# Loads spread over the attention's steps, x prepared group by group, and two reorderings of VectorE and GpSimd work

## The reference

```
# layer 0
xn = x * rsqrt(mean(x*x) + 1e-6);  q, k, v = split(xn @ w_qkv.T, 3)
q, k = rope(q), rope(k)                    # [x1*cos - x2*sin, x2*cos + x1*sin]
a = softmax(where(0 <= i - j <= 32, q k^T / 8, -1e9)) v
x = layernorm(x + a @ w_out.T);  x = layernorm(x + relu(x @ W1 + b1) @ W2 + b2)
# layer 1
k = k / norm(k);  A = tril(k k^T, -1) + I;  u = solve_triangular(A, v, lower=True)
x = layernorm-ed sum of x, (q k^T)(lr * u) @ out_w + out_b, and relu(ln(x) @ w1 + b1) @ w2 + b2
out = layernorm(x + light(x) + heavy(x of the 128 best tokens by coordinate descent))
```

## Time and profile before

| | us |
|---|---|
| median of 3 runs | 504.74 (504.71 to 506.62) |
| profiled execution | 509.57 |
| its span | 507.8 |
| PE / DVE / ACT / POOL busy | 399.8 / 321.9 / 255.8 / 179.1 |
| attention (first scores to end of its last output) | 22.9 to about 235 |
| delta stage | about 268 to 383 |
| MLP | about 383 to 413 |
| routing, feed-forwards, last norm | about 413 to 507.8 |

### The profile page before, as it was taken

The page is one execution under the profiler, slowest core; times in us unless marked ns, Lnnn a source line. Parts: engine busy times, 40 slices in busy tenths (PEclk is TensorE's granted clock), DMA queues, the critical chain, the costliest instruction groups (busy, mean ns, idle before and its releaser), DMA issues.

```text
span 507.8 us, 16578 instructions
## 1 busy us (share of the span) xinstructions
PE 399.8 (79%) x6608; PEld 351.6 (69%) x6608; DVE 321.9 (63%) x1552; ACT 255.8 (50%) x642; POOL 179.1 (35%) x194
## 2 busy tenths in 40 slices
PE   2778799999999999968998402999995668999940
PEld 1667698898998989956785302998983445787840
DVE  2688777777777777867258692222129961688845
ACT  3356545655665656655538300454401464678547
POOL 2733444545444444433535480000006780000004
PEclk9999999999999999999999855899997975999865
DMA  8378855556556465530200403000000000000002
GB/s 258 84 182 226 256 139 134 131 124 145 119 128 145 108 150 134 120 82 3 84 1 0 94 1 93 2 1 1 0 3 0 1 0 1 1 2 2 1 2 83
DMA packets 28861, 38.58 MB, mean 76 GB/s; under 512 B 8368, under 2 KB 20784, under 8 KB 28656
## 3 DMA queue, kind: packets, MB, share of 16 engines
q1 hardware_dynamic: 28496, 36.47, 29.4%
q10 hardware_dynamic: 288, 1.05, 0.5%
HBM read 8.93 MB, written 3.28 MB: 24 GB/s over the span
## 4 chain that ended last, share of the span: by engine, by line
PE 62%; DVE 15%; issue 6%; ACT 5%; POOL 4%; DMA 4%; SPq 3%; POOLq 0%; ACTq 0%; DVEq 0%
PE QK L545 9%; PE VY L618 5%; PE O L596 4%; PE S L572 4%; PE PT L582 3%; PE O L687 3%; PE QK L877 3%; PE PT L605 2%; DVE keys_T L1094 2%; PE QK L751 2%; PE O L759 2%; DMA t_swap<-t_sin 2%; SPq L460 2%; PE QK L857 2%; DVE unread_tests L1204 2%
## 5 line engine op out<-in xcount | busy, mean ns | idle before, releaser
L1516 POOL TENSOR_TENSOR qk<-t_cos,t_swap 128x512 f32<-128x512 f32 x64 | 80.3, 1275 | 110.3 <-DMA t_swap<-t_sin 100.1
L1293 ACT ACTIVATE probs<-probs,negative_max 128x64 f32<-128x64 f32 x256 | 68.0, 338 | 40.2 <-DVE negative_max L948 40.2
L939 DVE TENSOR_TENSOR t_cos<-QK,cos 128x512 f32<-128x512 f32 x64 | 43.9, 687 | 28.4 <-POOL qk L1516 16.2
L948 DVE CUSTOM_DVE_ANT_0 probs<-S,masks 128x64 f32<-128x64 f32 x256 | 39.5, 220 | 8.3 <-PE S L572 8.3
L939 DVE TENSOR_TENSOR t_sin<-QK,sin 128x512 f32<-128x512 f32 x64 | 43.6, 681 | 0.0
L1553 POOL TENSOR_TENSOR rstd<-var_eps,minus_half 128x4 f32<-128x4 f32 x24 | 25.3, 1055 | 37.6 <-DVE var_eps L992 32.8
L1314 ACT COPY oT<-PT 128x512 f32<-128x512 f32 x32 | 18.7, 584 | 38.3 <-PE PT L605 38.3
L545 PE MATMUL QK<-xnT,wq 128*128 128x128 f32 x256 | 36.1, 286 | 1.3 <-ACT xnT L1324 0.7
L618 PE MATMUL VY<-wo,oT 128*128 128x128 f32 x256 | 34.8, 279 | 1.3 <-ACT oT L1314 0.7
L596 PE MATMUL O<-v_before,probsT 64*32 64x65 f32 x1024 | 29.0, 225 | 8.7 <-issue 7.0
L545 PE MATMUL QK<-xnT,wk 128*128 128x128 f32 x256 | 35.1, 282 | 0.6 <-DVE t_sin L939 0.6
(11 more groups left out here) (272 smaller groups left out, 1098.8 us busy)
## 6 DMA issues: line engine op xcount, KB each, us to landing
t_swap<-t_sin SPq DMA_DIRECT2D x128, 128.0 KB
v_before<-v_own SPq DMA_DIRECT2D x32, 132.0 KB
v_before<-v_own SPq DMA_DIRECT2D x62, 66.0 KB
late_tile<-late_weights SPq DMA_DIRECT2D x1, 1513.0 KB, 7.6
x_sb<-x SPq DMA_DIRECT2D x4, 256.0 KB, 5.9
inverse_dram<-invT SPq DMA_DIRECT2D x1, 1024.0 KB, 5.1
gram_dram<-gram SPq DMA_DIRECT2D x4, 256.0 KB, 2.3
invT<-inverse_dram SPq DMA_DIRECT2D x4, 256.0 KB, 5.5
```

What stands on the lines that cost most here:

```text
L939: last = nc.vector.tensor_tensor(dst[:, u % G, PAIRS * j:PAIRS * j + PAIRS], QK[j][:].rearrange("p (m t) -> p m t", m=PAIRS), table[:, tok ...
L948: last = nc.vector.tensor_tensor_reduce(out=probs[:, u % G, m, e, :], in0=S[:, e, m, :], in1=masks[:, min(u // G, 1), :], scale=-1.0, scal ...
L1293: last = nc.scalar.activation(probs[:, u % G, m, e, :], probs[:, u % G, m, e, :], ACT.Exp, scale=-1.0, bias=negative_max[:, u % G, e, m:m ...
L1516: nc.gpsimd.tensor_tensor(qk[:, h, c, WINDOW:WINDOW + P], t_cos[:, h, c], t_swap[:, h, c], ALU.add).then_inc(rope_done, 1)
```

## The change

1. SyncE's loads. x's group 1 is loaded at the start, groups 2 and 3 in steps 4 and 12. The rope tables for tokens 512 and up come in three pieces of 512 tokens in steps 1, 9 and 17. late_tile comes in eight pieces in steps 9, 11, ... 23, and the five smaller loads in steps 24 to 26. wv and the second piece of the tables are issued earlier; wo is issued between the swaps of units 0 and 1.
2. Start. wq and wk are loaded and scaled in halves. The swap of unit 0 is issued in two parts, the q side and the k side, with eight DMAs. `split_x(0)` stands behind the rope products of units 0 and 1.
3. x by groups. XT_STEP = {2: 1, 10: 2, 18: 3} says in which step group q is transposed. normalise_x stands one step ahead of it, the squares two steps ahead (group 1: ahead of the loop), stage_x and split_x one step behind it, and GpSimd's inverse root ahead of the rope sum of that unit.
4. Keys' products. The masked copies of levels 1 and 2 move from GpSimd to VectorE, and they and weighted_keys stand behind the inversion. GpSimd's bias addition waits for weighted_keys.
5. MLP additions. GpSimd's first sum stands between the second and third root and waits for the first standardised group, the second between the third and fourth, the last two behind all four.

```diff
+    LATE_PIECES = 8
+    LATE_LOADS = 16 * (LATE_PIECES + 5)
+    XT_STEP = {UG * q - 6: q for q in range(1, TG)}
...
-            def swap_halves(u):
-                sp.wait_ge(rope_products_done, 2 * u + 2)
+            def swap_halves(u, sides=(0, 2)):
+                sp.wait_ge(rope_products_done, 2 * u + sides[1])
+                c = slice(PAIRS * sides[0], PAIRS * sides[1])
...
-            for q in range(2, TG):
-                load_x(q)
-            load_rope(1, slice(P, 4 * P))
-            for u in range(3):
-                swap_halves(u)
+            swap_halves(0, (0, 1))
+            swap_halves(0, (1, 2))
             sp.dma_start(wo[:], w_o.rearrange("(n p) c -> p n c", p=P)).then_inc(ld_wo, 16)
+            swap_halves(1)
+            swap_halves(2)
             for u in range(UNITS):
...
-                if u == 1:
-                    load_rope(2, slice(4 * P, T))
-                if u == 3:
-                    sp.dma_start(late_tile[:], late_weights).then_inc(ld_late, 16)
+                for q in range(1, TG):
+                    if u == UG * q - 7:
+                        load_rope(2, slice(512 * q, 512 * q + 512))
+                    if q > 1 and u == UG * q - 12:
+                        load_x(q)
+                if u % 2 == 1 and u // 2 in range(4, 4 + LATE_PIECES):
+                    w = late["end"][0] // LATE_PIECES
+                    c = slice(w * (u // 2 - 4), late["end"][0] if u // 2 == 3 + LATE_PIECES else w * (u // 2 - 3))
+                    sp.dma_start(late_tile[:, c], late_weights[:, c]).then_inc(ld_late, 16)
...
-                if 1 <= u < TG:
-                    transpose_x(u)
+                if u in XT_STEP:
+                    transpose_x(XT_STEP[u])
...
             normalise_x(0)
-            split_x(0)
...
+            split_x(0)
...
-                if u < TG - 1:
-                    normalise_x(u + 1)
-                if 2 <= u < TG + 1:
-                    split_x(u - 1)
+                if u + 1 in XT_STEP:
+                    normalise_x(XT_STEP[u + 1])
+                if u - 1 in XT_STEP:
+                    split_x(XT_STEP[u - 1])
...
+                if u > 0 and u + 2 in XT_STEP:
+                    squares(XT_STEP[u + 2])
...
-            inverse_rms(2, GB, NB)
             for u in range(UNITS):
+                if u in XT_STEP:
+                    q = XT_STEP[u]
+                    inverse_rms(q + 1, GB * q, GB * q + GB)
                 rope_sum(u)
...
-            pool.wait_ge(gram_done, TG)
-            for l in range(1, NLEV):
-                pool.wait_ge(quarters_masked, l)
-                nc.gpsimd.tensor_tensor(quarters_T[:, l], gram[:], level_mask[:, l:l + 1, :].broadcast_to([P, NB, P]),
-                                        ALU.mult).then_inc(quarters_masked, 1)
+            pool.wait_ge(weighted_keys_done, TG)
...
-            for q in range(TG):
-                inverse_root(q)
-            for q in range(TG):
+            def mlp_base(q):
                 pool.wait_ge(delta_added, q + 1)
                 nc.gpsimd.tensor_tensor(XC[:, grp(q)], XD[:, grp(q)], XE[:, grp(q)], ALU.add).then_inc(mlp_base_done, 1)
+            inverse_root(0)
+            for q in range(1, TG):
+                inverse_root(q)
+                if q < TG - 1:
+                    pool.wait_ge(mn_tokens_ready, q)
+                    mlp_base(q - 1)
+            pool.wait_ge(mn_tokens_ready, TG)
+            mlp_base(TG - 2)
+            mlp_base(TG - 1)
```

73 lines of the change are left out of this document (42 added, 31 removed).

## The result

The changed kernel takes 500.75 us (median of 5, 499.74 to 501.73), the kernel before in the same session 504.74 (median of 5, 504.60 to 508.42). The ratio is 0.990, 95% interval 0.9863 to 0.9938. It is faster, by 1.0% and not by the 2.8% forecast, and outside the range of 484 to 498.

A forecast was written before the change was run, and what follows sets the result against it. Bounds: TensorE's pace and waits in attention, VectorE beside GpSimd in the keys' products and MLP. Terms -11.6 - 2.6 + 0.4 - 7.7 + 5.8 + 1.5 = -14.2 took the median 504.74 to 490.5 us, range 484 to 498.

The forecast's parts named there:

- Keys' products: Keys' products and block inversion: inversion starts earlier, first products unslowed, moved products hidden; -11.6 us, bounds -13 and -8.6.
- Rival (d): Keys' products: the new order gives half, -11.6 becomes -6, total 496.1 us; chance 0.08.
- MLP additions: MLP: the last standardise no longer lies beside GpSimd's additions and ends earlier; -2.6 us, bounds -3.8 and -1.3.
- Start: Start to first scores: half swap lands 1.0 later, x maybe 0.5 earlier; +0.4 us, bounds -0.9 and +1.5.
- Steps 3 to 8: Attention: no large load queued there, so steps run at the later pace of 6.17 us; -7.7, bounds -8.1 and -3.2.
- x's groups: Attention steps 8 to 11 and 16 to 19: groups 2 and 3 cost 2.9 us each; +5.8, bounds +2.8 and +10.
- spread loads: Attention steps: 21 loads put into them, nearest to hidden; +1.5 us, ends 0 and +8.
- (b): Attention loses: groups at +10 and loads at +5, total 498.2 us; chance 0.21.
- (a): Attention: loads cost what they weigh, 25.7 us instead of 1.5, total 514.7, slower; chance 0.03.
- odd steps' scores wait for a rope sum regularly: Attention: sign that would prove the prediction wrong, an odd step's scores regularly waiting for GpSimd's rope sum.
- steps 9 to 26 over 6.6: Attention: sign that would prove the prediction wrong, these steps taking over 6.6 us in the mean.
- scores of step 9 some 7 us earlier: Attention: sign that would show the forecast, step 9's scores starting some 7 us earlier than before.

The follow-up runs named there:

- e4: The kernel before with only the two reorderings (keys' products and MLP additions), start and attention as before: 492.57 us, ratio 0.9730.
- e7: e4 plus the start alone: load order, first swap in halves, wo ahead of swaps 1 and 2: 495.38 us, ratio 0.9770.
- e17: The changed kernel with x's groups as before, wq and wk whole and split_x(0) first: 496.30 us, ratio 0.9822.
- e18: e11 plus x's groups, with x's loads in steps 4 and 12: 498.49 us, ratio 0.9866.
- e6: e4 plus x's groups moved into later steps, x still loaded in the start: 502.42 us, ratio 0.9899.
- e9: e6 with squares and roots of all groups kept in the start: 499.89 us, ratio 0.9860.
- e10: e9 with normalise_x placed behind the masks and the normalisation of the outputs: 499.72 us, ratio 0.9871.
- e8: The changed kernel with rope and late_tile pieces spread so no step has more than one piece: 498.12 us, ratio 0.9823.
- e5: e4 plus rope tables in three pieces, late_tile in eight and small loads in steps 24 to 26: 495.32 us, ratio 0.9774.
- e11: e4 plus late_tile in eight pieces and small loads in steps 24 to 26, rope tables whole: 491.12 us, ratio 0.9699.
- e2: The kernel before with the MLP additions' new order alone: 503.90 us, ratio 0.9937.
- e16: e11 with the five small loads in one step each, 24 to 28: 491.55 us, ratio 0.9680.

## Why the prediction was wrong, point by point

The terms of the two reorderings and of steps 3 to 8 held. What failed are the other terms of the attention: the way from step 0 to step 3, put at nothing, cost 3.4 us; the moved groups and the spread loads, put at 7.3 in steps 9 to 31, cost 9.8; and the sum, taken from one execution, was carried over to the median whole.

- **Keys' products** (-11.6): right, -12.1 in the traces and -12.9 alone. Blocks' landing 3.0 behind the issue, the first products at 0.2, and the moved products hidden all came as written. Rival (d) falls.
- **MLP additions** (-2.6): right, -2.4 and -3.2.
- **Start** (+0.4 on the first scores): right there. Not forecast were the 3.4 us from step 0 to step 3. Two sentences failed. The first is "wo now goes ahead of swaps 1 and 2, which the wait for the first rope sum hides": GpSimd waits 3.12 us for the swap behind wo where it waits 0.38 in e4, and its second rope sum starts at 26.36 for 23.18. With that start and the groups as before the stretch is as long (21.3 in e7, 21.7 in e17, for 18.5). The second is "with 0.4 for the split of group 1 that stays in step 3": I followed groups 2 and 3 and let group 1 move from step 1 to step 2 for nothing, where its normalisation meets rope sum 3 (3.12 us, TensorE idle 3.89, then half clock). With the old start that costs 0.2 to 1.9 (18.7 in e18, 19.9 to 20.4 in e6, e9 and e10). The meeting is not certain: in e8, with the changed kernel's own start, it did not come and the stretch took 19.3. I had the price of such a meeting in hand, 2.10 in the earlier trace rows, and the lock rule of the Trainium skill, "SBUF — State Buffer", section "Who interferes with whom", behind it. The trace agrees with the rule (3.12 beside 2.50 of GpSimd; four free ones took 1.11); I did not apply it to group 1.
- **Steps 3 to 8** (-7.7): right, -7.1. The stop went.
- **x's groups** (+5.8) **and spread loads** (+1.5): together +9.8 for +7.3 in steps 9 to 31, 2.5 too little. Both terms were mis-sized, and they do not add. Over e4, in steps 9 to 31, the groups alone are +8.5 (e6) and the loads alone +9.9 (e5), or +6.6 with the start (e17); all together are +10.8. For the groups the step that failed is "about half of the 2.10 + 1.1 of VectorE": 2.9 per group were forecast, e6 has 4.3, and 2.6 to 3 are reached only in e10, with squares and roots early and normalise_x behind the masks. For squares and root I had written down the queue and taken no price; what each of these is worth e9 and e10 do not tell beyond their error. For the loads the step that failed is "I cost it +1.5 in all, nearest to hidden". That their medians look cheap (e5 +2.2) is because the same kernels win back 4 us in steps 3 to 9. The pieces of late_tile alone cost nothing (e11), those of the rope tables alone 2.0 in the trace; only together, as the change has them, they cost 6.6 to 9.9, mostly as stops of TensorE and not as issue time on SyncE. The upper end of +8 was also too low: its 0.2 of transfer each comes from no row, and 4.37 MB in 21 loads at 324 GB/s are 0.64 each, so half of all of it would have been +13.
- **What a stop of TensorE costs.** None of the terms had the granted clock in it. I wrote of the slow step that it was "no clock effect"; the row I showed ended at 61.50, and the clock falls behind it. From 63.00 to 65.00 it is granted at 0.50, as the busy times of the kernel before show below. In e2, which keeps the late load too, the stop was 2.56, the clock stayed at 1.00 behind it, and the step took 8.7 and not 10.9.

```profile
61.10:63.00 1.90, 1.90 (x33) 1.81 (x33) 0.90 (x2) 0.88 (x4) 0.00 (x0) 0.79 1.09 312
63.00:65.00 2.00, 2.00 (x11) 2.00 (x11) 0.29 (x1) 0.69 (x3) 0.00 (x0) 0.50 1.11 236
```

- **From the profiled execution to the median.** Counted from the two traces this cost 4.5 of the 10.2 us by which the forecast missed, and the traces' own error 5.7. Counted by the ratios it nearly vanishes: 8.5 of 9.1 us are the attention's. The traces are 8.5 apart and the medians 4.0, since the profiled execution of before lay 4.8 above its median and that of the changed kernel 0.4. "I see nothing in the terms that belongs to those 4.8" was the sentence that failed as a way to argue. Single executions of the kernel before went from 502.35 to 512.0 in the sessions here, and the step with the late load took 8.7 to 14.7 us in the kernels that keep it (8.7 in e2, 10.9 in e4, 14.7 in e6). Against e4's trace, in a part where the two kernels are the same, that of before is 2.5 us longer (first masked product at 285.10 for 282.56). Whether a long stop was part of the 4.8 is not shown, since only the one execution of before has a trace.
- **The rivals.** (b), the attention loses, with 498.2 and a chance of 0.21, had the right place and was 2.6 short. It had neither wo nor group 1 nor the clock, and its terms for groups and loads (15 together, for 9.8) were above what steps 9 to 31 cost, so part of its nearness is luck. It put the attention 7.7 over the forecast; 6.8 was measured in the traces and 8.5 by the ratios. (a) falls: the loads do not cost the 25.7 that they weigh, at most 9.9. The mark "odd steps' scores wait for a rope sum regularly" did not come; the mark "steps 9 to 26 over 6.6" did: (197.3 - 83.4) / 17 = 6.7. Of what would show the forecast, "scores of step 9 some 7 us earlier" failed: they came 3.3 earlier, since the start had lost 3.4 more than forecast.

**A version that beats both.** Both reorderings with the late pieces and the small loads singly (e16) is at 0.968 (0.9632 to 0.9727), and e11 at 0.970, against 0.990 of the changed kernel. Their advantage over e4 (0.973) is inside the intervals; that over the changed kernel is not.

## What to carry to other kernels

Work moved out of a crowded start into a stage that one engine paces is not hidden because other engines have idle time there: count every link of its chain (squares, root, normalise, transpose, staging, split) at the queue that the pacing engine waits for, including the first of the moved pieces that shifts by only one step. Ask of every load that changes its place which small transfer now stands behind it, and who waits for that one. Price a stop of TensorE by what its granted clock does behind it, in a stretch that reaches past the stop. And compare kernels by many executions: a term that is sized from one execution that lay above its median cannot be taken whole from that median.
